# A 2:4 selection on the vector engine: comparisons kept as planes, nine instructions in place of thirteen

## The reference, cut to what matters

```python
def _sparsify_2to4(h):
    g = h.reshape(B, S, I // 4, 4)
    a = jnp.abs(g)
    _, idx = jax.lax.top_k(a, 2)
    mask = (pos == idx[..., 0:1]) | (pos == idx[..., 1:2])
    return (g * mask.astype(g.dtype)).reshape(B, S, I)

h = silu(x @ w_gate) * (x @ w_up)
out = _sparsify_2to4(h) @ w_down
x = x + out                       # x is layer-normalised first, then added back
```

## Time and profile before

| what | value |
|---|---|
| median of 3 runs | 1935.91 us (1935.52 to 1937.52) |
| the profiled execution's own time | 1935.51 us |
| its span in the profile | 1933.7 us |
| VectorE busy over the span | 1242.5 us (64%), 1979 instructions |
| TensorE busy over the span | 1764.7 us (91%), 8976 matmuls |
| sparse feed-forward phase | from about 1741 us to the end, 16 selections |

### The profile page before, as it was taken

The page is one execution under the profiler, slowest core; times in us unless marked ns, Lnnn a source line. Parts: engine busy times, 40 slices in busy tenths (PEclk is TensorE's granted clock), DMA queues, the critical chain, the costliest instruction groups (busy, mean ns, idle before and its releaser), DMA issues. The chain is left out here.

```text
span 1933.7 us, 29259 instructions
## 1 busy us (share of the span) xinstructions
PE 1764.7 (91%) x8976; PEld 1324.6 (69%) x8976; DVE 1242.5 (64%) x1979; ACT 1137.9 (59%) x2083; POOL 618.6 (32%) x501
## 2 busy tenths in 40 slices
PE   5999999998999999999989899779899799886997
PEld 4777777676786777777767688556557565555886
DVE  3655555554226555555644565788888788877997
ACT  2655655655126556556553354699995999953332
POOL 2232322222102223223220011029783087871000
PEclk9999999999999999999999899889999899998999
DMA  3000000000000000000001100012220122220000
GB/s 121 17 16 16 16 0 16 16 16 1 17 1 17 16 16 16 2 15 16 0 1 66 45 0 1 3 66 99 85 89 12 47 98 87 87 98 1 11 16 17
DMA packets 19959, 61.91 MB, mean 32 GB/s; under 512 B 2304, under 2 KB 6400, under 8 KB 19136
## 3 DMA queue, kind: packets, MB, share of 16 engines
q1 hardware_dynamic: 19904, 61.21, 9.0%
HBM read 58.84 MB, written 2.36 MB: 32 GB/s over the span
## 5 line engine op out<-in xcount | busy, mean ns | idle before, releaser
L1550 POOL TENSOR_SCALAR prob<-prob,rinv 128x128 f32<-128x128 f32 (+7 forms) x256 | 203.3, 794 | 687.2 <-DVE rinv L1160 685.4
L1618 POOL TENSOR_TENSOR m_h<-m_h,m_C 128x1024 f32<-128x1024 f32 x128 | 306.0, 2394 | 191.8 <-DVE m_h L1410 191.8
L1149 DVE TENSOR_SCALAR prob<-ps 128x128 f32<-128x128 f32 (+7 forms) x256 | 192.1, 750 | 240.3 <-PE ps L421 240.2
L456 PE MATMUL ps<-pt,v_sb 128*128 128x512 f32 (+3 forms) x768 | 319.9, 509 | 20.7 <-ACT pt L836 20.7
L1410 DVE TENSOR_TENSOR_SCAN m_h<-m_y,ps 128x1024 f32<-128x1024 f32 x128 | 291.5, 2284 | 50.8 <-PE ps L711 46.6
L836 ACT ACTIVATE pt<-ps 128x512 f32<-128x512 f32 (+3 forms) x384 | 182.1, 489 | 183.7 <-PE ps L445 181.2
L718 PE MATMUL ps<-m_h,ident 128*128 128x512 f32 x512 | 248.2, 608 | 11.1 <-POOL m_h L1618 11.1
L828 ACT ACTIVATE prob<-prob,nmax 128x128 f32<-128x128 f32 (+7 forms) x256 | 198.1, 774 | 81.5 <-DVE nmax L1154 80.4
L1154 DVE CUSTOM_DVE_ANT_0 prob<-prob,bias 128x128 f32<-128x128 f32 (+7 forms) x256 | 194.1, 758 | 44.3 <-issue 22.5
L1025 ACT ACTIVATE m_u<-m_uT,m_bT 128x256 f32<-128x256 f32 x512 | 210.6, 495 | 7.0 <-PE ps L711 6.9
L445 PE MATMUL ps<-ident,prob 128*128 128x128 f32 x1152 | 193.2, 276 | 15.2 <-POOL prob L1550 15.2
(11 more groups left out here) (197 smaller groups left out, 3083.0 us busy)
## 6 DMA issues: line engine op xcount, KB each, us to landing
m_C<-bc_dram SPq DMA_DIRECT2D x64, 512.0 KB, 3.6
wqk_raw<-wqk_in SPq DMA_DIRECT2D x16, 512.0 KB, 3.3
wv_raw<-wv_in SPq DMA_DIRECT2D x16, 256.0 KB, 3.5
x<-x_in SPq DMA_DIRECT2D x2, 1024.0 KB, 7.1
wo_sb<-wo_in SPq DMA_DIRECT2D x1, 2048.0 KB, 10.9
q_raw<-wgu_in SPq DMA_DIRECT2D x1, 2048.0 KB, 7.7
raw<-wgu_in SPq DMA_DIRECT2D x1, 2048.0 KB, 8.0
out<-x SPq DMA_DIRECT2D x8, 256.0 KB, 2.1
```

The source lines that it names most:

```text
L456: mm = nc.tensor.matmul(ps[:, 6 + g, r0 * P:BANK], v_sb[:, j, u * DH:(u + 1) * DH], pt[:, idx % 3, r0 * P:BANK], start=(j == 0), stop=(j = ...
L1149: nc.vector.tensor_scalar(tile, flat[:, o:o + n], CLIP, -CLIP, ALU.min, ALU.max).then_inc(s_read, 1)
L1550: nc.gpsimd.tensor_scalar(prob[:, at:at + n], prob[:, at:at + n], rinv[:, k:k + 1], 1.0, ALU.mult, ALU.mult).then_inc(norm_done, 1)
L1618: nc.gpsimd.tensor_tensor(state, state, m_C[:, v, :], ALU.mult).then_inc(hc_done, 1)
```

## The change

The change rewrites `sparse` and its scratch tensors. The magnitudes and `f_h` are now seen with the place in front, [128, 4, 256], so that an operand such as `a[:, 0:3, :]` runs through place 0 of all 256 groups, then place 1, then place 2; the data itself lies in memory as before, so neighbouring elements of that order are 16 bytes apart. The scratch tensors are real planes: 256 neighbouring bfloat16 values for each place.

- The three comparisons have the same sizes (768, 512, 256); their results go into `c_near` and `c_far`. The last is `<` and not `>=`.
- Two additions of 512 elements take the place of three (512, 256, 256).
- Three comparisons (256, 256, 512) build the four planes of `keep`; before there were two additions and two comparisons of 256.
- One multiplication of 1024 elements takes the place of three instructions (256, 256, 512).
- `f_step` is counted 7 times a tile in place of 9. There are three waits for it as before.

```diff
-                a = f_abs[:, j, :].rearrange("p (g e) -> p g e", e=4)
-                h = f_h[:, j, :].rearrange("p (g e) -> p g e", e=4)
+                a = f_abs[:, j, :].rearrange("p (g e) -> p e g", e=4)
+                h = f_h[:, j, :].rearrange("p (g e) -> p e g", e=4)
...
-                did(nc.vector.tensor_tensor(c1[:, :, :], a[:, :, 0:3], a[:, :, 1:4], ALU.is_ge))
-                did(nc.vector.tensor_tensor(c2[:, :, :], a[:, :, 0:2], a[:, :, 2:4], ALU.is_ge))
-                did(nc.vector.tensor_tensor(c3[:, :], a[:, :, 0], a[:, :, 3], ALU.is_ge))
+                did(nc.vector.tensor_tensor(c_near[:, 0:3, :], a[:, 0:3, :], a[:, 1:4, :], ALU.is_ge))
+                did(nc.vector.tensor_tensor(c_far[:, :, :], a[:, 0:2, :], a[:, 2:4, :], ALU.is_ge))
+                did(nc.vector.tensor_tensor(c_near[:, 3, :], a[:, 0, :], a[:, 3, :], ALU.is_lt))
                 settle()
-                did(nc.vector.tensor_tensor(u12[:, :, :], c1[:, :, 0:2], c2[:, :, :], ALU.add))
-                did(nc.vector.tensor_tensor(t2[:, :], c1[:, :, 1], c2[:, :, 0], ALU.add))
-                did(nc.vector.tensor_tensor(v3[:, :], c1[:, :, 2], c2[:, :, 1], ALU.add))
+                for i in range(2):
+                    ins = nc.vector.tensor_tensor(c_sum[:, 2 * i:2 * i + 2, :], c_near[:, i:i + 2, :], c_far[:, :, :],
+                                                  ALU.add)
+                did(ins)
                 settle()
-                did(nc.vector.tensor_tensor(w0[:, :], u12[:, :, 0], c3[:, :], ALU.add))
-                did(nc.vector.tensor_tensor(w3[:, :], v3[:, :], c3[:, :], ALU.add))
-                nc.vector.tensor_tensor(k12[:, :, 0], u12[:, :, 1], c1[:, :, 0], ALU.is_gt)
-                did(nc.vector.tensor_tensor(k12[:, :, 1], c1[:, :, 2], t2[:, :], ALU.is_ge))
+                did(nc.vector.tensor_tensor(keep[:, 0, :], c_sum[:, 0, :], c_near[:, 3, :], ALU.is_gt))
+                did(nc.vector.tensor_tensor(keep[:, 1, :], c_sum[:, 1, :], c_near[:, 0, :], ALU.is_gt))
+                did(nc.vector.tensor_tensor(keep[:, 2:4, :], c_near[:, 2:4, :], c_sum[:, 2:4, :], ALU.is_ge))
                 settle()
-                nc.vector.scalar_tensor_tensor(h[:, :, 0], w0[:, :], 1.5, h[:, :, 0], ALU.is_ge, ALU.mult)
-                nc.vector.scalar_tensor_tensor(h[:, :, 3], w3[:, :], 1.5, h[:, :, 3], ALU.is_le, ALU.mult)
-                nc.vector.tensor_tensor(h[:, :, 1:3], k12[:, :, :], h[:, :, 1:3], ALU.mult).then_inc(f_sp, 1)
+                nc.vector.tensor_tensor(h, keep[:, :, :], h, ALU.mult).then_inc(f_sp, 1)
```

More of the change, by code:

```diff
@@ L150, in program @@
         f_abs = place(mem, "f_abs", [P, 2, F])
[L151 to L159, removed]
+        c_near = place(mem, "c_near", [P, 4, F // 4], BF16)
+        c_far = place(mem, "c_far", [P, 2, F // 4], BF16)
+        c_sum = place(mem, "c_sum", [P, 4, F // 4], BF16)
+        keep = place(mem, "keep", [P, 4, F // 4], BF16)
         mem.close()
@@ L1257, in settle @@
                 def settle():
-                    dve.wait_ge(f_step, (p - first) * 18 + (9 * j + step[0]))
+                    dve.wait_ge(f_step, (p - first) * 14 + (7 * j + step[0]))
                 dve.wait_ge(f_absd, (p - first) * 2 + (j + 1))
```

## The result

| | median | runs |
|---|---|---|
| before | 1936.98 us | 1935.52 to 1937.83, 10 runs |
| changed | 1942.05 us | 1938.07 to 1943.02, 10 runs |

The ratio is 1.0024, with a 95% interval of 1.0015 to 1.0033: slower by 5 us, just over the 3.9 us that the prediction took as the least that can be told from no change. The forecast of 1938.1 us was 4 us too low; 1942.05 us lies within the stated range of 1932 to 1948 us, but outside the forecast's own bounds of 1935.4 to 1939.2 us.

The account below looks back on a forecast made before the run. VectorE was taken to bound the last phase, TensorE close behind. A selection's parts summed to 6.55 us against 6.39, 0.16 longer; 16 tiles add 2.6 us to 1935.51, giving 1938.1 us, range 1932 to 1948.

Parts of the forecast that it names:

- VectorE sets the period, TensorE is 1.1 us behind: Last phase's loop body of 20.50 us: VectorE has no gap left, TensorE has 1.1 us of waits.
- All 16 selections on the path when longer: Sparse phase: nothing hides a longer selection, so 0.16 us each over 16 tiles adds 2.6 us.
- Price (a): VectorE's selection: float32 elements 16 bytes apart cost 0.18 us extra for every 256, growing with the elements.
- first comparison: Selection's comparison of 768 elements, now strided: 1.41 us start to start, 0.87 before.
- second comparison: Selection's comparison of 512 elements, now strided: 0.96 us start to start, 0.60 before.
- multiplication: Selection's final 1024 elements, strided on one input and the output: 1.86 us start to start, 1.65 before.
- Price (b): Selection's additions and mask comparisons: as dense bfloat16, 256 further elements cost 0.13 us.
- additions and masks: Selection's dense bfloat16 part: two additions 0.80 us (1.26 before), three mask comparisons 0.87 us (1.36 before).
- The stated ends: Range of one selection's length, 6.39 to 6.62 us, giving 1935.4 to 1939.2 us in total.
- R1: Strided comparisons and multiplication: fixed part hidden, every 256 elements cost 0.51 us; 0.60 us a tile longer, 1945.1 us; chance 0.18.
- R2: Mask comparisons not done at the packed bfloat16 rate: 0.69 us a tile longer, 1946.5 us; chance 0.12.
- R3: Strided instructions pay 180 ns once each, not per element: selection 5.47 us, TensorE would bound, 1926.1 us; chance 0.14.

Follow-up runs that it names:

- the second execution: The changed kernel run once more, unedited, in a later call: 1942.15 us, ratio 1.0027 to the kernel before.
- the probe: Changed kernel plus nine scratch VectorE instructions behind each selection of tile 0, mostly 1024 elements, dense or strided; ran once, 2056.35 us.

## Why the prediction was right or wrong, point by point

- **VectorE sets the period, TensorE is 1.1 us behind.** Right in kind. The size of TensorE's slack was wrong: the period could fall by 1.64 us (20.50 to 18.86), which two runs showed.
- **All 16 selections on the path when longer.** Right in sum: 16 x 0.27 = 4.3 us against 4.2 in the phase and 5.1 in the medians. It holds selection by selection for the ten of the five periods; of the last three only about half showed in the time (0.4 us of 0.8, and 0.3 in the second execution), and the first three cost more than their own length (1.1 us for 0.8, and 1.3).
- **Price (a), 0.18 us for every 256 strided elements.** Right that it grows with the elements; the size was a little low. It was (1562 - 955) / 3 = 0.20 for the first comparison, where 955 is what L1263 took in the bodies of the kernel before, (1062 - 685) / 2 = 0.19 for the second, and (1998 - 1226) / 4 = 0.19 for the multiplication.
- **Price (b), packing.** Right: 421, 284 and 418 ns; by starts 0.79 and 0.87 us for additions and masks, where 0.80 and 0.87 stood.
- **The mis-sized terms.** By starts, the means of all 16: first comparison 1.48 where 1.41 stood, multiplication 1.90 where 1.86 stood, second comparison 0.98 where 0.96 stood. The sum was 6.66 us and not 6.55. It was a small difference of two large ones, 1.11 lost and 0.95 saved, so 7% on the 1.62 us that price (a) makes in it turned 0.16 into 0.27. The stated ends, 6.39 and 6.62 us, came from the multiplication alone; the comparisons had no range, and the first of them missed by the most.
- **Where the 4 us came from.** 1.5 us is the base: the prediction added to 1935.51 us, the profiled execution, and the median of ten is 1936.98. 1.7 us is the selection, 4.3 for 2.6. The other 0.8 us is not accounted for; the interval of the ratio is wider than that. The prediction gave "same" 0.47 and "slower" 0.35, and at 0.24%, over its own bound of 0.2%, the less likely of the two came. That the time lies in the stated range is in part luck: the range reached to 1948 for the sake of R1 and R2, and neither came true as stated.
- **R1** (no fixed part left in a strided instruction) came true in part for the comparisons: by starts 1.48 lies about half way from 1.41 to its 1.53, and 0.98 a third of the way from 0.96 to its 1.02, but 1.90 is far from its 2.12 for the multiplication. Its reason falls: the first 128 strided elements took 383 ns and the next 128 took 225, so 158 ns are fixed, as in dense instructions (157). After these 157 ns the second comparison costs 1.77 ns an element, like the 1024 of the probe; why the 768 of the first cost 1.83 stays open.
- **R2** fell: dense comparisons are packed. **R3** fell: 225 ns from 128 to 256 elements, 0.7 ns an element above the dense rate.
- **The Trainium skill's rule of 16-byte lines** ("SBUF — State Buffer", section "SBUF: two separate sides"), by which two or more hits in a line run at full rate, was borne out for float32 inputs: no surplus at 8 bytes apart (692 ns for 512), a full one at 16 and at 32 (383 and 387 ns for 128); outputs were tried at 16 bytes only, with a full surplus. The same section puts the free stride at four float32 or eight bfloat16 elements. The measurements decide otherwise: four float32 elements are 16 bytes and cost the surplus, and for two-byte writes four elements (8 bytes) apart, 1024 of them cost 2426 ns where dense unpacked elements of that number would cost about 1.22 us, as the float32 ones did.

## What to carry to other kernels

Fewer instructions are worth about 0.07 us each here, a float32 element without a neighbour in its 16 bytes costs 0.7 ns, so 100 such elements outweigh an instruction. Count strided elements before instructions, and when planes are wanted, make the data come out in planes, by the order of the weights' columns, instead of viewing it so. When a forecast is the difference of two large terms, give the range of each term and not only of the largest. A busy time of an engine that has gaps is no floor for the period; leave the work of the other engine out to see the floor. A sum of durations also misses what longer waits do to TensorE's granted clock.

## What the runs showed of the hardware that was not expected

- A float32 tensor_tensor of 1024 elements pays about once for a stride of 16 bytes: 1968, 1964 and 1962 ns with one input, both inputs or the output strided, and 1998 with one input and the output (the changed kernel's multiplication), against 1221 dense. All three at once was not tried.
- Two-byte results written apart: 725 ns for 512 at 4 bytes, about 728 for 256 at 8 bytes, 724 for 128 at 16 bytes, and 3676 ns for 768 scattered over planes 512 bytes apart, 4.6 ns each beside the fixed 157 ns.
- ScalarE's magnitude of 1024 float32 elements with an input 16 bytes apart: 2101 ns against 1056.
- The granted clock fell to 0.50 (1.2 GHz) just after TensorE had stood idle for 2.3 us in the run with float32 scratch; in the bodies of the changed kernel, with idle stretches of 1.3 us, it stayed at 1.00.
